# Second attention: the order in which the transfers of the query and key stacks walk their rows

## The chip, the cores and the metric

The kernel runs on one core of a Trainium2 chip. The metric is the time of one execution on the device in microseconds (us), smaller is better. TensorE is called PE below, VectorE DVE, ScalarE ACT, GpSimd POOL and SyncE SP; SP computes nothing and issues transfers (DMAs).

## What is computed

Four layers follow each other, each with a residual and a layer norm: an attention over 16 batches of 512 tokens, a routed feed-forward layer, a second attention, another routed feed-forward layer. The change touches the second attention alone:

```
q = q.reshape(B, S, HEADS, HEAD_DIM)      # 16 heads of 8
k = k.reshape(B, S, HEADS, HEAD_DIM)
logits = jnp.einsum('bihd,bjhd->bhij', q, k) * scale + pos_bias[None]
attn = jax.nn.softmax(logits, axis=-1)
out = jnp.einsum('bhij,bjhd->bihd', attn, v).reshape(B, S, D)
```

## The kernel before

The program has five stages; `attention_two` is the third. It works through 16 batches (`bodies`), each of 4 groups (j = 0 to 3) of 4 heads. A group has 16 tiles (4 heads times 4 blocks of tokens), so a batch has 64.

The query and the key are float32. They are split into three bfloat16 parts each (`split`), whose sum is the value, and the product of query and key is made of the parts that matter: high, middle and low key with the high query, the same with the middle query, high and middle key with the low query. That is 8 pairs of parts, and with a head dimension (`HD`) of 8 it makes 64 rows to contract over. `kst` and `qst` ("stacks") hold these 64 rows of keys and queries, for two heads of a pair on the two halves of the 128 partitions (`HALF`). They are filled through memory: `put_parts` writes the parts to `parts_d`, and `stack(s, j)` reads them back into the rows of group j of batch s. There is one `kst` and one `qst` for all batches.

`stack` issues 12 transfers on SP's queue: for each of two halves three for `kst` and three for `qst`, of 24, 24 and 16 rows (3, 3 and 2 parts times 8 dimensions) of 2 KB each. For `kst` the source walks over the parts; for `qst` it names one part again and again, with a step of 0 (`walks` is False). In the kernel before the rows of a transfer are ordered part first, head dimension second. All twelve signal `stack_in{j}`.

On SP a body runs, in this order: `stack(s, 3)` (from batch 1 on), the load for batch s+2, `tops(s, 1)`, `put_parts(s+1)`, `stack(s+1, 0)`, `tops(s, 2)`, the store of batch s-1, `stack(s+1, 1)`, `tops(s, 3)`, `clear_rows` (2 MB of zeros), `stack(s+1, 2)`, `tops(s+1, 0)`. Ahead of the bodies stand `put_parts` and all four `stack` of batch 0, and behind them `tops(0, 0)`. SP does these strictly one after the other, with their waits.

`tops(s, j)` carries the maxima of the rows of scores: it waits until DVE has made `mT` (`m_ready`, L1786), writes it to `tops_d`, waits for that to land, and reads it with four transfers into `line` (named `spread_line` in the profile).

PE runs over 32 slots of two tiles in each body. In each slot it makes `scores` (L1419, c_s) for tiles 32 ahead, then `below` (L1427) and `biased` (L1437, c_u) for the tiles of the slot, and `values` (L1451, c_o). DVE reads the scores and keeps their maxima (L1781), ACT the exponentials (L1628). Three waits tie PE to SP: `scores` of the first tile of a group waits for `stack_in{j}`, `biased` of the first tile of a group waits for `m_in{j}` of `tops`, and, the other way round, `stack(s, j)` waits for the last `biased` of group j of the batch before, since it overwrites what that reads.

Of the kernel before, what the change touches and what calls it, by code (L numbers as in the profile page):

```python
# [20 lines left out]
NB, N, W = 16, 512, 128  # L21
T = N // P
H, A = 16, 64
# [5 lines left out]
HD = W // H  # L29
# [45 lines left out]
def need(eng, sem, n):  # L75

    if not (isinstance(n, int) and n <= 0):
        eng.wait_ge(sem, n)


def apart(eng, passed):


    eng.sem_inc(passed, 1)
# [1029 lines left out]
def attention_two(nc, g, keep):  # L1114
# [4 lines left out]
    PARTS = 3  # L1119
    HALF = P // 2  # L1120
    PAIRS = H // 2
    GP = G // 2
# [14 lines left out]
    def sem(name):  # L1137
        return g.sem(f"c_{name}")

    with ExitStack() as ctx:  # L1140
        def sb(name, shape, dt=F32):
            return ctx.enter_context(nc.sbuf_tensor(f"c_{name}", shape, dt))
# [15 lines left out]
        rows = sb("rows", [P, T], U32)  # L1158
        st = sb("st", [P, T, 6])
# [86 lines left out]
        with nc.Block() as block:  # L1246

            @block.sync
            def _(sp):
# [15 lines left out]
                def stack(s, j):  # L1265

                    for w in range(2):
                        sp.wait_ge(sem(f"parts_out{w}"), 16 * s.b + 16)
                        apart(sp, sem("sp_passed"))
                    need(sp, sem("u_ps"), ALL * (s.b - 1) + TILES * (j + 1))  # L1270
                    apart(sp, sem("sp_passed"))
                    part = P * N
                    for half in range(2):
                        for st, w, walks in ((kst, 1, True), (qst, 0, False)):
                            for a in range(PARTS):
                                rows = HD * (PARTS if a < PARTS - 1 else PARTS - 1)
                                src = bass.AP(io["parts_d"].tensor,
                                              (2 * s.par + w) * PARTS * part + (0 if walks else a * part) + (half * PAIRS + j * GP) * N,
                                              [[part if walks else 0, rows // HD], [H * N, HD], [1, GP * N]])
                                at_row = HALF * half + a * PARTS * HD  # L1280
                                sp.dma_start(st[at_row:at_row + rows, GP * j:GP * j + GP, :].rearrange("r h n -> r (h n)"), src
                                             ).then_inc(sem(f"stack_in{j}"), 16)

                def tops(s, j):
# [23 lines left out]
                def body(s, on):  # L1308
                    if not isinstance(s.b, int) or s.b > 0:
                        stack(s, 3)  # L1310
                    if on.front:
                        load(s.ahead().ahead())
                    tops(s, 1)
                    if on.nxt:
                        put_parts(s.ahead())
                        stack(s.ahead(), 0)
                    tops(s, 2)
                    if on.tail:
                        store(s.back())
                    if on.nxt:  # L1320
                        stack(s.ahead(), 1)
                    tops(s, 3)
                    clear_rows(sp, "zs_d", s.b, io, sem("rows_clear"))
                    if on.nxt:
                        stack(s.ahead(), 2)
                        tops(s.ahead(), 0)
# [977 lines left out]
```

## Time and profile before

| | us |
|---|---|
| median of 3 runs | 2276.47 |
| the runs | 2275.68, 2276.47, 2283.36 |
| the profiled execution | 2270.51 |
| its span (first to last instruction) | 2268.7 |

The stage of the second attention runs from about 762 to 1990 us of the span. In the profile "c_" stands ahead of its tiles. An SP row of the timeline gives the time at which SP began to issue a transfer, and how long the issuing took; the transfer itself goes on behind it. SP rows of equal names that follow each other are merged into one ("x3"). A wait is shown as idle time in brackets with what ended it. L84 is the line at which SP waits inside a helper.

### The profile page before, as it was taken

To read this page: it belongs to the slowest core of one execution; us is meant where nothing else is said; L and a number is where in the kernel's file an instruction comes from. 1 tells how busy PE (TensorE), PEld (TensorE's weight loads), DVE (VectorE), ACT (ScalarE), POOL (GpSimd) and SP (SyncE) were. 2 spreads that over 40 slices of the span, in tenths; PEclk is the share of its full clock that TensorE was granted. 3 is DMA by queue.
4 is the path that set the end of the run, shared out by engine and by line. 5 is a ranking of instruction groups with operands and counts; after the bars stand their busy time and mean duration, and the time that the engine had idled before them with its cause. 6 is when DMAs were issued, how large, how long until landed. Compare 5 with 4: busy or idle time off the path is not lost. (4 is left out here: it accounts for less than half of the span.)

```text
span 2268.7 us, 46879 instructions
## 1 busy us (share of the span) xinstructions
PE 1857.9 (82%) x15436; PEld 953.6 (42%) x15436; DVE 1481.3 (65%) x4594; ACT 1076.7 (47%) x2723; POOL 800.9 (35%) x811
## 2 busy tenths in 40 slices
PE   8477878777568588898898988988888999679896
PEld 6255556555446323333333333333333333246554
DVE  6268878887521376786778777786677777233277
ACT  3355655556123235555555555555555565323221
POOL 4458888888510212122221222122221220100166
PEclk9689999999789779999999999999999999889999
DMA  3553322332168323332333234332333332144333
GB/s 110 161 186 107 108 87 89 110 107 96 35 190 242 113 78 108 94 114 74 110 98 111 70 110 116 95 114 72 109 95 113 86 97 82 59 134 163 127 98 98
DMA packets 147093, 247.66 MB, mean 109 GB/s; under 512 B 20628, under 2 KB 49316, under 8 KB 146356
## 3 DMA queue, kind: packets, MB, share of 16 engines
q1 hardware_dynamic: 137828, 220.80, 31.7%
q0 software_dynamic: 9072, 24.41, 3.9%
q8 instruction: 105, 1.72, 0.3%
q14 instruction: 88, 0.72, 0.1%
HBM read 198.16 MB, written 121.96 MB: 141 GB/s over the span
## 5 line engine op out<-in xcount | busy, mean ns | idle before, releaser
L1781 DVE CUSTOM_DVE_ANT_0 c_sums<-c_s,bias 128x512 f32<-128x512 f32 x1024 | 663.5, 686 | 249.1 <-PE c_s L1419 176.5
L1628 ACT ACTIVATE c_pT<-c_u 128x512 f32<-128x512 f32 x1024 | 571.7, 596 | 510.7 <-PE c_u L1437 425.6
L1437 PE MATMUL c_u<-spread_line,c_pick 128*32 128x512 bf16 x4096 | 325.1, 395 | 38.5 <-DMA spread_line<-tops_d 38.4
L1451 PE MATMUL c_o<-c_pT,c_vst 128*32 128x256 f32 x4096 | 319.5, 389 | 14.5 <-ACT c_pT L1628 11.3
L1419 PE MATMUL c_s<-c_kst,c_qst 64*128 64x512 bf16 x1024 | 242.5, 402 | 23.5 <-DVE c_tops L1781 18.7
L1427 PE MATMUL c_u<-c_qst,c_kst 64*128 64x512 bf16 x1024 | 227.9, 388 | 25.3 <-issue 12.7
L521 ACT ACTIVATE v<-a_bank,gain 128x64 f32<-128x64 f32 x768 | 165.7, 344 | 54.4 <-DVE vp L735 54.3
L1451 PEld LDWEIGHTS c_o<-c_pT,c_vst 128*32 128x32 f32 x4096 | 122.3, 112 | 139.0 <-issue 30.4
L1375 POOL DMA_INDIRECT zs_d<-c_xs,c_slot x64 | 63.2, 988 | 303.9 <-DMA zs_d<-in_zeros 255.1
L387 PE MATMUL a_bank<-wv,xT 128*128 128x512 f32 x256 | 154.6, 691 | 18.9 <-ACT v L521 14.4
L1437 PEld LDWEIGHTS c_u<-spread_line,c_pick 128*32 128x32 bf16 x4096 | 62.1, 95 | 240.8 <-issue 191.7
L588 POOL TENSOR_TENSOR q<-q,vp 128x1024 f32<-128x1024 f32 x48 | 125.0, 2603 | 104.7 <-DVE vp L735 103.6
L1419 PEld LDWEIGHTS c_s<-c_kst,c_qst 64*128 64x128 bf16 x1024 | 59.1, 93 | 214.8 <-DVE c_tops L1781 104.5
L599 POOL TENSOR_TENSOR s<-q,v 128x1024 f32<-128x1024 f32 x48 | 143.0, 2979 | 0.2
L529 ACT COPY oT<-a_bank 128x512 f32<-128x512 f32 x128 | 69.5, 586 | 148.4 <-PE a_bank L408 148.3
L735 DVE TENSOR_TENSOR vp<-a_bank,ez 128x512 f32<-128x512 f32 x96 | 64.9, 687 | 102.1 <-PE a_bank L387 100.3
L416 PEld LDWEIGHTS a_bank<-wo,oT 128*128 128x128 f32 x1024 | 123.8, 195 | 14.3 <-issue 14.3
L416 PE MATMUL a_bank<-wo,oT 128*128 128x128 f32 x1024 | 126.2, 277 | 0.0
L751 DVE TENSOR_TENSOR o<-o,r 128x1024 f32<-128x1024 f32 x64 | 124.3, 1961 | 0.0
L2075 POOL DMA_INDIRECT e_routed<-us_d,rows x64 | 62.8, 981 | 171.9 <-POOLq L2191 154.3
L408 PE MATMUL a_bank<-ident,o 128*128 128x128 f32 x512 | 79.8, 306 | 52.9 <-DVE o L751 52.2
L1364 POOL TENSOR_TENSOR c_rstd<-c_ve,minus_half 128x4 f32<-128x4 f32 x16 | 16.7, 1045 | 278.6 <-DVE c_ve L1750 278.6
(263 smaller groups left out, 2900.3 us busy)
## 6 DMA issues: line engine op xcount, KB each, us to landing
xs_d<-in_zeros SPq DMA_DIRECT2D x16, 2048.0 KB
zs_d<-in_zeros SPq DMA_DIRECT2D x16, 2048.0 KB
spread_line<-tops_d SPq DMA_DIRECT2D x256, 64.0 KB
parts_d<-c_parts SPq DMA_DIRECT2D x32, 384.0 KB
c_kst<-parts_d SPq DMA_DIRECT2D x256, 48.0 KB
c_qst<-parts_d SPq DMA_DIRECT2D x256, 48.0 KB
d_w<-in_wd SPq DMA_DIRECT2D x24, 384.0 KB
b_w<-in_wb SPq DMA_DIRECT2D x24, 321.0 KB
```

Source lines behind the costliest of these rows:

```text
L387: nc.tensor.matmul(v_ps[h][:], xT[s.par][:, t, :], wv[:, 512 * h:512 * h + 512], start=True, stop=True).then_inc(sem("v_ready"), 1)
L416: mm = nc.tensor.matmul(y_ps[:, t * W:(t + 1) * W], oT[t % 2][:, k, :], wo[:, k, :], start=(k == 0), stop=(k == HA // P - 1))
L521: ins = nc.scalar.activation(dst[:, h * A:(h + 1) * A], v_ps[half][:, k * A:(k + 1) * A], ACT.Copy, scale=gain[s.par][:, t, h:h + 1])
L588: nc.gpsimd.tensor_tensor(q[:, t, :], q[:, t - 1, :], vp[t % 2][:], ALU.add).then_inc(sem("q_ready"), 1)
L599: nc.gpsimd.tensor_tensor(s1[s.par][:, t, :], q[:, t - 1, :], v2[t % 2][:], ALU.add).then_inc(sem("s1_ready"), 1)
L751: v.tensor_tensor(heads(o[t % 2][:]), heads(o[t % 2][:]), r[s.par][:, t, :].unsqueeze(2).to_broadcast([P, H, A]), ALU.mult).then_inc(sem(" ...
L1419: nc.tensor.matmul(s_ps[bank_of(n)][:], qst[rows_of(h), h // 2, t * P:(t + 1) * P], kst[rows_of(h), h // 2, :], start=True, stop=True).the ...
L1427: nc.tensor.matmul(u_ps[bank_of(n)][:], kst[rows_of(h), h // 2, c * P:(c + 1) * P], qst[rows_of(h), h // 2, :], start=True, stop=False, sk ...
L1437: mm = nc.tensor.matmul(u_ps[bank_of(n)][ARRAY * k:ARRAY * (k + 1), :].rearrange("k (t q) -> k t q", t=T), pick[:, c, k, :], line[:, G * j ...
L1451: mm = nc.tensor.matmul(o_ps[ARRAY * i:ARRAY * (i + 1), half * 2 * P:(half + 1) * 2 * P], vst[s.par][:, c, f:f + ARRAY], pT[r % 2][:, i, h ...
L1628: nc.scalar.activation(pT[n // G % 2][:, n % G, :], u_ps[bank_of(n)][:], ACT.Exp).then_inc(sem("exp_done"), 1)
L1781: v.tensor_tensor_reduce(sums[n % 2][:], s_ps[bank_of(n)][:], bias, 1.0, -3.0e38, ALU.add, ALU.max, top_s[j % 2][:, k:k + 1]).then_inc(sem ...
```

## The change

The source of each transfer of `stack` is described with the head dimension outermost and the part second, instead of the part outermost and the head dimension second. `kst` and `qst` are reordered in the same way, so each product sums the same 64 terms in another order. The number of transfers, their sizes and their destinations stay.

```
-                                rows = HD * (PARTS if a < PARTS - 1 else PARTS - 1)
+                                n = PARTS if a < PARTS - 1 else PARTS - 1
                                 src = bass.AP(io["parts_d"].tensor,
...
-                                              [[part if walks else 0, rows // HD], [H * N, HD], [1, GP * N]])
+                                              [[H * N, HD], [part if walks else 0, n], [1, GP * N]])
                                 at_row = HALF * half + a * PARTS * HD
-                                sp.dma_start(st[at_row:at_row + rows, GP * j:GP * j + GP, :].rearrange("r h n -> r (h n)"), src
+                                sp.dma_start(st[at_row:at_row + n * HD, GP * j:GP * j + GP, :].rearrange("r h n -> r (h n)"), src
```

No engine but SP has another order, and on SP no instruction moves: what changes is the form of some. Below, a row is a transfer with its line, what it writes and reads, and the form of its destination (rows x elements of 2 bytes; a 1 between them is a dimension that the destination is given to match a source of three dimensions).

SP ahead of the bodies, the parts of batch 0 (`parts_d`) and the first half of `stack(0, 0)`, before:

```order
L1262 DMA parts_d<-c_parts 128x3x512 x2
L1281 DMA c_kst<-parts_d 24x1024 x2
L1281 DMA c_kst<-parts_d 16x1024
L1281 DMA c_qst<-parts_d 24x1x1024 x2
L1281 DMA c_qst<-parts_d 16x1x1024
```

The same place after:

```order
L1262 DMA parts_d<-c_parts 128x3x512 x2
L1281 DMA c_kst<-parts_d 24x1x1024 x2
L1281 DMA c_kst<-parts_d 16x1x1024
L1281 DMA c_qst<-parts_d 24x1x1024 x2
L1281 DMA c_qst<-parts_d 16x1x1024
```

Before, the source of `kst` is one even walk over 24 (or 16) rows, since a part is exactly 8 rows further on than the part ahead of it: two dimensions fall into one. With the head dimension outermost they don't, and `kst` gets the form that `qst` has had.

SP in a body, the second half of `stack(s+1, 1)`, then `tops(s, 3)` and the zeros, before:

```order
L1281 DMA c_kst<-parts_d 24x1024 x2
L1281 DMA c_kst<-parts_d 16x1024
L1281 DMA c_qst<-parts_d 24x1x1024 x2
L1281 DMA c_qst<-parts_d 16x1x1024
L1290 DMA tops_d<-c_mT 16x256
L1300 DMA spread_line<-tops_d 8x4x1024 x4
L172 DMA zs_d<-in_zeros 128x8x512
```

And after:

```order
L1281 DMA c_kst<-parts_d 24x1x1024 x2
L1281 DMA c_kst<-parts_d 16x1x1024
L1281 DMA c_qst<-parts_d 24x1x1024 x2
L1281 DMA c_qst<-parts_d 16x1x1024
L1290 DMA tops_d<-c_mT 16x256
L1300 DMA spread_line<-tops_d 8x4x1024 x4
L172 DMA zs_d<-in_zeros 128x8x512
```

Nothing moved; `tops` stands behind the same twelve transfers.

## Rows read from the trace of the kernel before

**Rows 1.** The page, part 1: busy time and share by engine.
```profile
PE 1857.9 (82%) x15436; PEld 953.6 (42%) x15436; DVE 1481.3 (65%) x4594; ACT 1076.7 (47%) x2723; POOL 800.9 (35%) x811
```
**Rows 2.** Busy time by stretch (us, then PE, PEld, DVE, ACT, POOL, clock, DMA share, GB/s).
```profile
788.00:860.00 72.00, 56.72 (x411) 15.92 (x411) 48.38 (x163) 23.47 (x49) 12.20 (x15) 0.73 0.29 77
860.00:1900.00 1040.00, 926.92 (x10146) 348.51 (x10146) 775.31 (x2867) 580.13 (x1179) 234.59 (x261) 0.97 0.35 100
```
**Rows 3.** Waits of PE, 860 to 1900 us: us in total, times, longest.
```profile
PE c_u L1437 <- DMA spread_line<-tops_d: 26.3, 16, 3.5
PE c_s L1419 <- DVE c_tops L1781: 17.0, 27, 2.7
```
**Rows 4.** Waits of PE, 788 to 860 us.
```profile
PE c_u L1437 <- DMA spread_line<-tops_d: 7.8, 2, 4.7
...
PE c_s L1419 <- DMA c_qst<-parts_d: 0.8, 1, 0.8
```
**Rows 5.** Line 1281, issues on SP: duration in ns, min/median/max.
```profile
L1281 SPq DMA_DIRECT2D c_kst<-parts_d x384: 4/357/1478, 788.5 to 1902.8; - x192
L1281 SPq DMA_DIRECT2D c_qst<-parts_d x384: 619/689/870, 789.6 to 1904.7; - x192
```
**Rows 6.** Other lines that issue on SP, the same columns.
```profile
L1300 SPq DMA_DIRECT2D spread_line<-tops_d x256: 88/301/545, 818.9 to 1942.9; - x128
...
L172 SPq DMA_DIRECT2D zs_d<-in_zeros x16: 667/677/697, 867.4 to 1943.2; - x16
...
L177 SPq DMA_DIRECT2D zs_d<-in_zeros x1: 648/648/648, 820.2 to 820.2; - x1
...
L320 SPq DMA_DIRECT2D bias_d<-line_d x16: 855/2952/4026, 48.9 to 91.2; - x16
```
**Rows 7.** DMA packets while one stack is filled, 1053.3 to 1062.5 us.
```profile
DMA packets 353, 0.54 MB, mean 59 GB/s; under 512 B 96, under 2 KB 96, under 8 KB 352
...
q1 hardware_dynamic: 352, 0.52, 17.7%
```
**Rows 8.** Timeline of SP at the stage's start: first and last pieces of four stacks.
```profile
788.46 1.13 SPq L1281 DMA_DIRECT2D c_kst<-parts_d  x3
789.63 2.24 SPq L1281 DMA_DIRECT2D c_qst<-parts_d  x3
...
814.16 2.08 SPq L1281 DMA_DIRECT2D c_qst<-parts_d  x3
816.42 0.31 SPq L1290 DMA_DIRECT2D tops_d<-c_mT  x1
```
**Rows 9.** Timeline of DVE, 811 to 817 us: the maxima of group 0, batch 0.
```profile
812.37 0.27 DVE L1786 TENSOR_TENSOR c_mT<-c_misc,c_mT 16x128 bf16<-16x128 f32 x1
```
**Rows 10.** Timeline of PE: the first scores, the first biased, group 2 of batch 0.
```profile
798.72 1.03 PE L1419 MATMUL c_s<-c_kst,c_qst 64*128 64x512 bf16 x3 [0.85 <-DMA c_qst<-parts_d]
...
824.62 1.04 PE L1437 MATMUL c_u<-spread_line,c_pick 128*32 128x512 bf16 x8 [4.67 <-DMA spread_line<-tops_d]
...
856.37 0.62 PE L1437 MATMUL c_u<-spread_line,c_pick 128*32 128x512 bf16 x8 [3.17 <-DMA spread_line<-tops_d]
```
**Rows 11.** Timeline of SP ahead of group 2, batch 0.
```profile
846.22 2.09 SPq L1281 DMA_DIRECT2D c_qst<-parts_d  x3
848.49 0.31 SPq L1290 DMA_DIRECT2D tops_d<-c_mT  x1
```
**Rows 12.** Waits of SP, 860 to 1900 us.
```profile
SPq L84 <- DVE c_mT L1786: 118.7, 46, 5.2
```
**Rows 13.** Timeline of SP, a group 3 and a group 2 late in the stage.
```profile
1731.26 2.09 SPq L1281 DMA_DIRECT2D c_qst<-parts_d  x3
1736.66 0.31 SPq L1290 DMA_DIRECT2D tops_d<-c_mT  x1
...
1786.05 2.09 SPq L1281 DMA_DIRECT2D c_qst<-parts_d  x3
1789.45 0.31 SPq L1290 DMA_DIRECT2D tops_d<-c_mT  x1
```
**Rows 14.** Timeline of PE at the same two groups.
```profile
1743.39 0.61 PE L1437 MATMUL c_u<-spread_line,c_pick 128*32 128x512 bf16 x8 [1.35 <-DMA spread_line<-tops_d]
...
1797.15 0.61 PE L1437 MATMUL c_u<-spread_line,c_pick 128*32 128x512 bf16 x8
```

## The prediction

> **What bounds the kernel now.** I began with the page's busy shares: PE is the busiest engine [rows 1]. Cut by stretch, the steady part of the second attention keeps PE busy for 926.92 of 1040 us, ahead of DVE with 775.31; the first 72 us of the stage are looser, 56.72 us busy [rows 2]. So in this stage a microsecond counts when PE loses it. The second view is therefore PE's waits. Of what this change touches, the steady part shows one wait: `biased` for the transfers of `tops`, 26.3 us in 16 waits, about one in each batch, and none for `kst` or `qst` [rows 3]. At the start of the stage there are two such waits for `tops`, 7.8 us, and one of 0.8 us for a stack [rows 4]. The landing of the stacks is thus hardly waited for. But SP issues a stack's twelve transfers one after the other ahead of nearly every `tops`, so the time that the *issuing* takes can reach PE by way of `tops`. The last view is thus SP's timeline: is SP early or late when DVE has the maxima ready?
>
> **The price of issuing.** A `kst` transfer takes SP 0.357 us, a `qst` transfer 0.689 us (0.619 at the least) [rows 5]. They have the same rows of 2 KB and differ in form: the source of `kst` is one even walk, that of `qst` has two dimensions against a destination that has one. Three `qst` with the gaps between take 2.09 us, three `kst` between 1.1 and 1.2, and a whole stack 6.65 us (four stacks: 788.46 to 814.16 + 2.08 = 816.24, or 27.8 us with the waits between them [rows 8]). After the change all twelve have two dimensions against one. No row shows that form with 8 outermost. The bounds are the nearest rows [rows 6]: `spread_line`, which has 8 outermost on both sides and equal dimensions, 0.301 us; the transfers of zeros, 0.648 and 0.677 us; `bias_d`, with 7 outermost, whose first and cheapest issue took 0.855 us (the others queue up behind its own packets). I take 0.65, between `qst`'s cheapest and its median, as `qst` is the nearest form; its 24 and 16 rows (0.69 and 0.62) have 3 and 2 outermost, and 8 may go like either. With gaps of 0.045 us a stack is then 12 x 0.695 = 8.3 us, +1.65 us. Ends: 12 x 0.345 = 4.1 us (-2.5) and 12 x 0.90 = 10.8 us (+4.2).
>
> **The landings.** The transfers of `qst` spread their rows over more of the 16 DMA engines, those of `kst` over fewer. A stack moves 256 rows with 96 small packets beside them in 9.2 us, 17.7% of the engines' time [rows 7]: 0.177 x 16 x 9.2 / 352 = 0.074 us a packet. Were the last transfer of a stack to put 2 rows on an engine instead of 8, the stack would land 6 x 0.074 = 0.4 us sooner behind its issue. In the steady part nobody waits for that, as no such wait stands in [rows 3]; at the start it can give back 0.4 of the 0.85 us that the first scores wait [rows 10]. I leave it out of the sum, as the issue ahead of it grows by more.
>
> The Trainium skill (DMA: Bandwidth & Descriptors, "Why a DMA increments its semaphore by 16 and not by 1") states that such a transfer runs on as many engines as the largest number up to 16 that divides the outermost dimension of both sides. That makes 12, 12 and 16 for `kst` and 3, 3 and 2 for `qst`, twice 48 small packets, and the trace agrees with its 96 [rows 7]; it makes 8 for every transfer after. By that rule alone one would forecast a gain.
>
> **The sum, place by place.**
> 1. *Start of the stage.* The four stacks of batch 0 stand in a row ahead of `tops(0, 0)`. They end at 816.24; DVE had the maxima at 812.37 + 0.27 = 812.64 [rows 9], 3.6 us earlier, and SP goes on at 816.42 [rows 8]. PE starts `biased` 8.2 us later, at 824.62, after 4.67 us of waiting that this transfer ended [rows 10]. So SP is on the path here, and it grows by 4 x 1.65 = 6.6 us. PE's first scores start some 1 us later too, but DVE then has 3.6 us in hand. Nothing covers the 6.6 us: everything after follows from PE's first `biased`.
> 2. *Group 2 of batch 0.* `stack(1, 0)` ends at 848.31, `tops` follows at 848.49, without a wait in between [rows 11], and PE waits 3.17 us for it [rows 10]. Another 1.65 us.
> 3. *The steady part.* Here SP is early: it waits for DVE's maxima 46 times, 118.7 us in all, 2.6 us on average [rows 12]. A stack that takes 1.65 us longer eats into that. At group 3, where PE waits once in a batch (1.35 us at 1743.39 [rows 14]), SP is done at 1733.35 and begins `tops` at 1736.66: 3.3 us, of which 0.17 is the step itself; no cost [rows 13]. Group 2 is the tightest: at 1788.14 to 1789.45 SP had 1.1 us in hand, and there 0.5 us would come through; PE didn't wait at that group and has some tenths of its own [rows 13, 14]. In that stretch I count five groups with less than 1.65 us in hand (1.1 to 1.6), some 1.5 us of lateness together, of which PE's own room takes a third: +1.0 us. Group 1 has 2.4 us in hand and as much again on PE's side, group 0 more.
>
> Queued behind the longer stacks on SP are also the load for the batch after next, the store and the zeros; PE and POOL show no wait that a delay of 1.65 us there would lengthen on the path to PE.
>
> Sum: 6.6 + 1.65 + 1.0 = +9.25 us. On the profiled execution (2270.51 us, its span 2268.7 and 1.8 around it) that gives 2279.8; the median of the runs stands 6.0 us above the profiled one, and gives 2276.47 + 9.25 = 2285.7 us, +0.4%.
>
> **The rivals.**
> - *The form is dear with more engines.* If issuing pays for each outermost step in this form, as 0.62 for 2, 0.69 for 3 and 0.855 for 7 could be read, a stack is 10.8 us, +4.2. Then the start costs 16.8, group 2 of batch 0 4.2, and in the steady part group 2 comes out late by 4.2 - 2.6 = 1.6, about 1.1 on PE, and group 3 by 4.2 - 3.1 = 1.1, in 14 batches each: 31 us. Total +52, 2328 us. It starts to bite where a stack passes 9.3 us. Against it speak the zeros: 16 and 128 outermost at 0.65 and 0.68 [rows 6].
> - *Faster: 8 outermost is the cheap form.* If what makes `qst` dear is 3 and 2 as outermost dimension, and not the second dimension, all twelve cost what `spread_line` costs, 0.301 us [rows 6], and a stack is 4.1 us. SP then passes the start 10 us sooner, but DVE's maxima hold it at 812.64: 3.6 us gained, 0.8 with earlier first scores, 2.5 at group 2 of batch 0, nothing in the steady part, where DVE sets the time of `tops`. -6.9 us, 2269.6. It decides for faster from a mean issue below 0.51 us. Against it: the zeros have powers of two outermost and are dear.
> - *Nothing to be seen.* `kst` stays at 0.36 us and `qst` gets no dearer, or its gain and `kst`'s loss cancel; the landing gives 0.4 us: 2276. This is also where the skill's rule on engines alone would lead, since no wait of PE but the first hangs on a stack's landing.
>
> **How the numbers follow.** The forecast's price (0.62 to 0.70, +7 to +11.5 us) has 62%, the dear form 14%, the cheap form 6%, nothing to be seen 16%, something else 2%. The range leaves out the dear form's end and little below: 2274 (an execution's scatter under "nothing") to 2298 (a stack of 9.3 us: 4 x 2.65 + 2.65 + 5, and a few us of scatter). A measurement of this kernel can tell about 0.5%, 11.4 us, from no change. Within that lie the cheap form, nothing, and four fifths of the forecast; slower by more are the rest of it and the dear form: slower 0.28, same 0.70, faster 0.02.
>
> **What would show it.** In the profile after: `kst`'s median issue at line 1281 near 0.65 us (0.36: nothing; 0.9: dear; 0.3: cheap), `qst`'s near 0.65 too; SP's last stack of batch 0 ending near 823 instead of 816.24, PE's first `biased` near 831 with some 11 us of waiting; PE's waits for `spread_line` in 860 to 1900 us (shifted) at 27 to 29 us; small packets beside a stack again 96. The prediction falls if the issue price stays outside 0.5 to 0.75, or if PE makes up for a late start later in the batch.

## The result

The changed kernel takes 2298.39 us (median of 4 runs, 2291.08 to 2299.05), the kernel before 2276.07 us (4 runs, 2275.42 to 2283.36). The ratio is 1.0083, 95% interval 1.0054 to 1.0112. It is slower by more than can be confused with no change, and the 22.3 us are 2.4 times the 9.25 that were forecast. On two other chips the same pair gave 1.0122 (1.0089 to 1.0155) and 1.0120 (1.0084 to 1.0156); these intervals overlap with the first.

The profiled execution took 2291.08 us (span 2289.2), 20.6 us more than that of before. Issuing at line 1281, after (duration in ns, min/median/max), beside [rows 5]:

```profile
L1281 SPq DMA_DIRECT2D c_kst<-parts_d x384: 484/650/1617, 794.7 to 1921.9; - x192
L1281 SPq DMA_DIRECT2D c_qst<-parts_d x384: 642/643/1356, 797.0 to 1923.9; - x192
```

`kst` went from 0.357 to 0.650 us, `qst` from 0.689 to 0.643. A stack of twelve takes 8.28 us (median of 64) instead of 6.68. Waits of PE, first from 794 to 872 us, then from 872 to 1912 us, which answer to [rows 4] and [rows 3]:

```profile
PE c_u L1437 <- DMA spread_line<-tops_d: 13.8, 2, 10.9
...
PE c_s L1419 <- DMA c_qst<-parts_d: 0.7, 1, 0.7
```
```profile
PE c_u L1437 <- DMA spread_line<-tops_d: 34.4, 24, 2.9
PE c_s L1419 <- DVE c_tops L1781: 18.6, 30, 1.7
```

The longest of the first group grew from 4.7 to 10.9 us, and in the steady part there are 24 waits with 34.4 us instead of 16 with 26.3. SP's own waits in the steady part (872 to 1912 us) show where its time in hand went: 50.5 us in 32 waits for DVE's maxima, against the 118.7 us in 46 of [rows 12].

```profile
SPq L84 <- PE c_u L1437: 101.0, 28, 9.8
SPq L84 <- DMA parts_d<-c_parts: 65.6, 28, 4.5
SPq L84 <- DMA tops_d<-c_mT: 62.8, 40, 3.3
SPq L84 <- DVE c_mT L1786: 50.5, 32, 5.2
```

The start of the stage in the timelines of SP, DVE and PE, after, beside [rows 8 to 10]:

```profile
794.72 2.25 SPq L1281 DMA_DIRECT2D c_kst<-parts_d  x3
797.01 2.02 SPq L1281 DMA_DIRECT2D c_qst<-parts_d  x3
...
827.54 2.02 SPq L1281 DMA_DIRECT2D c_qst<-parts_d  x3
829.73 0.35 SPq L1290 DMA_DIRECT2D tops_d<-c_mT  x1
```
```profile
818.49 0.27 DVE L1786 TENSOR_TENSOR c_mT<-c_misc,c_mT 16x128 bf16<-16x128 f32 x1
```
```profile
836.98 1.04 PE L1437 MATMUL c_u<-spread_line,c_pick 128*32 128x512 bf16 x8 [10.89 <-DMA spread_line<-tops_d]
```

SP now ends the four stacks at 829.56, 10.8 us behind DVE's maxima (818.76); it was 3.6 us.

**Where the time is.** The stage cut at points of the timelines (us): from the issue of the first load of the stage to the first `kst`, from there to the first `biased`, from that to the one of batch 1, from that to the one of batch 15, and from there to the last store. The chips are numbered in the order of use; "old form" is the row order of before.

| kernel, chip | stage begins | to first kst | to first biased | to batch 1 | batch 1 to 15 | first kst to last store |
|---|---|---|---|---|---|---|
| before, 1 | 762.4 | 26.1 | 36.2 | 65.5 | 1009.7 | 1183.4 |
| after, 1 | 768.6 | 26.1 | 42.3 | 65.8 | 1014.7 | 1197.1 |
| start_only, 2 | 782.0 | 26.1 | 42.6 | 66.2 | 949.2 | 1131.1 |
| after_again, 2 | 771.7 | 26.2 | 42.6 | 66.2 | 967.0 | 1148.7 |
| before_again, 3 | 766.8 | 26.1 | 37.0 | 66.9 | 940.2 | 1116.2 |
| after_third, 4 | 768.0 | 26.2 | 42.0 | 65.8 | 969.9 | 1149.7 |

On chip 1, 13.7 of the 20.6 us lie inside the stage: 6.1 at its start and 5.0 between batches 1 and 15, 2.3 from the first `biased` of batch 15 on. 6.2 us lie ahead of it, in stages that the change doesn't touch.

### The profile page after: what moved, and what is told of

Its sections match the earlier page's. It is cut to its first block and busy times, and to the rows that moved or that the text cites. A ratio compares the mean times of both kernels' runs of the same rounds, so it can differ in the third digit from the quotient of the medians.

```text
span 2289.2 us, 46879 instructions
## 1 busy us (share of the span) xinstructions
PE 1866.4 (82%) x15436; PEld 959.7 (42%) x15436; DVE 1485.3 (65%) x4594; ACT 1079.8 (47%) x2723; POOL 801.2 (35%) x811
## 5 line engine op out<-in xcount | busy, mean ns | idle before, releaser
L1419 PE MATMUL c_s<-c_kst,c_qst 64*128 64x512 bf16 x1024 | 242.9, 404 | 24.8 <-DVE c_tops L1781 20.2
L416 PEld LDWEIGHTS a_bank<-wo,oT 128*128 128x128 f32 x1024 | 128.9, 202 | 14.4 <-issue 14.4
L751 DVE TENSOR_TENSOR o<-o,r 128x1024 f32<-128x1024 f32 x64 | 132.2, 2085 | 0.0
L416 PE MATMUL a_bank<-wo,oT 128*128 128x128 f32 x1024 | 131.0, 284 | 0.0
L1364 POOL TENSOR_TENSOR c_rstd<-c_ve,minus_half 128x4 f32<-128x4 f32 x16 | 16.7, 1045 | 275.2 <-DVE c_ve L1750 275.2
```

The source lines that it names most:

```text
L416: mm = nc.tensor.matmul(y_ps[:, t * W:(t + 1) * W], oT[t % 2][:, k, :], wo[:, k, :], start=(k == 0), stop=(k == HA // P - 1))
L751: v.tensor_tensor(heads(o[t % 2][:]), heads(o[t % 2][:]), r[s.par][:, t, :].unsqueeze(2).to_broadcast([P, H, A]), ALU.mult).then_inc(sem(" ...
L1419: nc.tensor.matmul(s_ps[bank_of(n)][:], qst[rows_of(h), h // 2, t * P:(t + 1) * P], kst[rows_of(h), h // 2, :], start=True, stop=True).the ...
```

## The experiments

Every kernel below was timed beside the kernel before on the same chip (2, 3 or 4, as the tables say), and each ratio is to that. The table is worked out from their timelines in one way: for groups 1 to 3 of batches 1 to 14, **in hand** is the time from the end of SP's last issue ahead of `tops` to the end of DVE's L1786 (negative where SP is late), **write to read** the time from the start of the issue of `tops_d` to that of the first `spread_line`, both means in us, and **PE waits** the sum of PE's idle time just ahead of the group's first `biased`. Where the text gives a mean for group 0, it is over batches 1 to 15.

| kernel, chip | in hand, g1 | g2 | write to read, g1 | g2 | PE waits g1 | g2 | g3 |
|---|---|---|---|---|---|---|---|
| before, 1 | 1.95 | 2.28 | 1.85 | 1.58 | 0.0 | 0.3 | 24.1 |
| after, 1 | 0.25 | -0.36 | 2.63 | 2.01 | 0.3 | 8.1 | 24.4 |
| start_only, 2 | 1.98 | 0.07 | 2.04 | 2.66 | 4.5 | 7.4 | 24.0 |
| after_again, 2 | 0.27 | -1.77 | 2.56 | 2.00 | 8.4 | 20.7 | 25.4 |
| after_load_moved, 2 | 0.70 | -1.28 | 1.82 | 2.09 | 1.9 | 14.0 | 24.8 |
| before_again, 3 | 1.94 | 0.24 | 1.97 | 2.32 | 3.8 | 3.4 | 23.8 |
| before_padded, 3 | 0.75 | -1.74 | 2.93 | 3.04 | 13.1 | 34.8 | 24.8 |
| eight_parts, 3 | 6.12 | 1.20 | 1.91 | 2.11 | 4.6 | 3.1 | 25.0 |
| after_third, 4 | 0.25 | -1.69 | 2.56 | 2.06 | 9.9 | 20.4 | 24.4 |
| issue_only, 4 | 0.21 | -1.79 | 3.01 | 2.59 | 13.0 | 28.8 | 25.5 |

### Twice the same kernels: after_again, after_third, before_again

> The changed kernel once more, with more rounds, since its profiled execution is 20.6 us longer and 6.3 of these lie ahead of the second attention, in stages that the change doesn't touch. Theory (SP's issue time, all inside the second attention: start +6, steady part +8): ratio 1.005 to 1.007, and the stage begins at 762 to 764 us as before. Rival (something of the whole program is slower after the change, such as its placement in memory): the stage begins near 768 us again and the ratio is 1.008 to 1.010.

> The changed kernel once more, so that it shares a chip with the next ones. By the two calls so far (ratios 1.008 and 1.012 on two chips): 1.008 to 1.014, PE's waits for spread_line in the steady part 8 to 26 us above those of the kernel before.

> The kernel before, unchanged, for a trace of it from the same chip as the other kernels of this call. Ratio 1.000 within its interval by every theory. Its use: the second attention from the first biased of batch 1 to that of batch 15 takes as long as with the old form in start_only (949 us on that chip, 1010 us on the first one), if the chip's own pace explains the difference between the two chips.

The changed kernel gave 1.0122 (1.0089 to 1.0155) and 1.0120 (1.0084 to 1.0156), above what the first expectation's theory and its rival allowed; the kernel before against itself 0.9982 (0.9963 to 1.0002). The stage of the changed kernel began at 771.7 us in after_again, where 762 to 764 and 768 were expected, and at 768.0 in after_third; but kernels that are the same up to there began it anywhere from 760.0 to 783.4. So the 6.2 us ahead of the stage on chip 1 are scatter of the stages ahead, and nothing of the change. The loss on chip 2 is inside the stage: between batches 1 and 15 the changed kernel takes 967.0 us where start_only, which has the old form there, takes 949.2.

Those chips run this part quicker (67 to 69 us a batch against 72), before and after. In the kernel before, SP has 0.24 us in hand at group 2 on chip 3 and 2.28 on chip 1, and as much at groups 1 and 3 on both within 0.2 us. PE's waits at group 2 grow by 13.3 us on chip 2 (start_only to after_again) and by 7.8 on chip 1. That fits a smaller room for the longer stacks on the quicker chips, but the ratios of chips 1 and 2 differ by 0.4% with an uncertainty of as much, so that the loss is larger there isn't shown by the runs.

### One part alone: start_only

```
-                                              [[H * N, HD], [part if walks else 0, n], [1, GP * N]])
+                                              [[H * N, HD], [part if walks else 0, n], [1, GP * N]] if s.b == 0 else
+                                              [[part if walks else 0, n], [H * N, HD], [1, GP * N]])
```

> The new row order for the four stacks of batch 0 alone, the old one for all later batches. Theory: four stacks of 8.3 instead of 6.65 us stand on the path once: first biased +6.2 us against the stage's begin, the steady waits of PE for spread_line stay at 26 us, ratio 1.0027 (+6 us). Rival (a slower engine split, 8 engines for all, matters for landings in every batch): most of the loss is in the later batches, and this kernel is at +1 us or less.

Ratio 1.0024 (1.0000 to 1.0047), 5.3 us; from the first `kst` to the first `biased` 42.6 us, as in after_again, against 37.0 in before_again. The start's term holds on its own. PE's steady waits for `spread_line`, 26 us in the expectation, are 35.9 in the table's groups: that number was chip 1's. The rest of the change's 1.2% on that chip comes from later batches.

### SP on the path at the start: after_stack3_moved

```
-                for j in range(GROUPS):
+                for j in range(GROUPS - 1):
                     stack(at(0), j)
                 tops(at(0), 0)
+                stack(at(0), GROUPS - 1)
```

> The changed kernel with the last stack of batch 0 issued behind the first tops instead of ahead of it. Its rows are wanted only some 20 us later. Theory: SP is 10.8 us late at the first tops; one stack less ahead of it takes 8.3 us off, PE's wait at the first biased falls from 10.9 to some 2.7 us and the time by 8 us against the changed kernel: ratio to the kernel before 0.999 to 1.004. Rival (the start's delay is made up for later in the batch): the wait goes, the time stays.

Ratio 1.0087 (1.0060 to 1.0114), above the 0.999 to 1.004 that were expected, since the changed kernel itself stands at 1.0122 on this chip and not at 1.008. It is 0.35% or 7.8 us below after_again on the same chip, with an uncertainty of 0.4%, so the runs alone don't show the gain; the traces do. The first `biased` comes 33.0 us after the first `kst` instead of 42.6; 1.6 us of that are given back in batch 0 (67.8 instead of 66.2 us to batch 1). Waits of PE up to 870 us in after_again, then in this kernel:

```profile
PE c_u L1437 <- DMA spread_line<-tops_d: 11.3, 1, 11.3
```
```profile
PE c_u L1438 <- DMA spread_line<-tops_d: 4.6, 2, 3.2
```

Of the 4.6 us 1.4 are at the first `biased`. So in these traces only those 1.6 us of the start are made up for later, and the change's delay there goes by a move of twelve transfers that nobody wanted yet.

### The load ahead of the small write: after_load_moved

```
-                    if not isinstance(s.b, int) or s.b > 0:
-                        stack(s, 3)
                     if on.front:
                         load(s.ahead().ahead())
+                    if not isinstance(s.b, int) or s.b > 0:
+                        stack(s, 3)
```

> The changed kernel with the load of 256 KB for the batch after next issued ahead of the stack of group 3, instead of right ahead of the tops of group 1. Theory: with longer stacks SP comes to that tops without slack, so its small write is issued 0.9 us behind the load instead of 2.5 and lands 1.8 to 3.6 us later; this and two longer stacks in a row make SP late at group 2. With the load out of the way the write takes 1.3 us again, PE's waits for spread_line in the steady part fall from 34.4 us in 24 waits to 26 to 29 in 16 to 18, and the time by 5 to 8 us against the changed kernel. Rival (it is the longer stacks alone): the waits fall by 2 us or less.

This came out of a comparison of SP's timeline at group 1. The kernel before, and after, in the same batch:

```profile
1332.43 0.41 SPq L1252 DMA_DIRECT2D c_x<-x_d  x1
1334.75 0.31 SPq L1290 DMA_DIRECT2D tops_d<-c_mT  x1
1336.35 1.30 SPq L1300 DMA_DIRECT2D spread_line<-tops_d  x4
...
1344.08 1.12 SPq L1281 DMA_DIRECT2D c_kst<-parts_d  x3
```
```profile
1345.88 0.44 SPq L1252 DMA_DIRECT2D c_x<-x_d  x1
1346.51 0.32 SPq L1290 DMA_DIRECT2D tops_d<-c_mT  x1
1348.90 1.30 SPq L1300 DMA_DIRECT2D spread_line<-tops_d  x4
...
1356.19 2.07 SPq L1281 DMA_DIRECT2D c_kst<-parts_d  x3
...
1362.43 2.02 SPq L1281 DMA_DIRECT2D c_qst<-parts_d  x3
1364.64 0.34 SPq L1290 DMA_DIRECT2D tops_d<-c_mT  x1
```

Before, the small write of `tops` stands 2.3 us behind the load of 256 KB and its read can start 1.6 us later. After, it stands 0.6 us behind, and that takes 2.4 us. Everything up to the next stack shifts by that, the stack is 1.6 us longer itself, and SP reaches the `tops` of group 2 late, without a wait. PE then waits where it did not (timeline of PE, after):

```profile
1373.14 0.61 PE L1437 MATMUL c_u<-spread_line,c_pick 128*32 128x512 bf16 x8 [0.89 <-DMA spread_line<-tops_d]
```

With the load moved the ratio is 1.0041 (1.0018 to 1.0064), 0.8% or 18 us below after_again, and batches 1 to 15 take 949.2 us, as in start_only. The write to read of group 1 falls from 2.56 to 1.82 us, PE's waits at groups 1 and 2 from 29.1 to 15.9 us. These numbers are above what was expected in us, and the count of waits (35, with 46.9 us) is not down to the expected 18; that had been reckoned from chip 1. The move also takes 0.5 us of issuing out of the chain, and how the 18 us divide between that and the quicker write isn't shown. The rival, that it is the longer stacks alone, is out: their length is the same in both (8.27 us), and PE's waits at groups 1 and 2 fell by 13 us where it allowed 2. The DMA packets show the write held up: at group 1 of batches 1 to 13 the last packets ahead of it end 1.6 us after its issue in after_again (0.4 in after_load_moved), and its own last packet at 1.9 us (1.2).

### The form without the 8 engines: before_padded

```
-                        sp.dma_start(io["parts_d"][s.par, w].rearrange("a p n -> p a n"), parts[w][:]
+                        sp.dma_start(io["parts_d"][s.par, w, :, 0:P].rearrange("a p n -> p a n"), parts[w][:]
...
-                    part = P * N
+                    part = (P + 1) * N
...
-"parts_d": ([2, 2, 3, P, N], BF16)
+"parts_d": ([2, 2, 3, P + 1, N], BF16)
```

> The kernel before with one unused row block between the parts in memory. The row order stays part first, but the key's source is no longer one even walk, so its transfers get the form of the query's, on 3 and 2 engines instead of 12 and 16; the 8 engines of the change are not in it. Theory (the issue time alone counts): kst issues at 0.69 and 0.62 us, a stack takes 8.5 us, the first biased comes 7 us later after the stage's begin, batches 1 to 15 take as much longer as in the changed kernel, ratio 1.009 to 1.014 on the chip of the last call. Rival (the number of engines or the later landing matters): the ratio differs from the changed kernel's by 0.4% or more, either way.

Issuing at line 1281:

```profile
L1281 SPq DMA_DIRECT2D c_kst<-parts_d x384: 619/672/881, 786.1 to 1906.8; - x192
L1281 SPq DMA_DIRECT2D c_qst<-parts_d x384: 619/675/1004, 788.5 to 1908.9; - x192
```

The stack is 8.44 us, as long as the changed kernel's 8.28 within 0.2, and the ratio is 1.0386 (1.0357 to 1.0415): three times the change's loss. My theory at that point, that the issue time alone counts, fell. Waits of SP in the steady part, in before_again and then here:

```profile
SPq L84 <- DMA tops_d<-c_mT: 110.3, 61, 3.5
```
```profile
SPq L84 <- DMA tops_d<-c_mT: 151.6, 55, 5.7
```

SP waits longer for its own small write to land, 2.8 instead of 1.8 us on average, up to 5.7. With 3, 3 and 2 engines for each transfer of `kst` and `qst`, those few still work through the stack when the write arrives: at group 2 the stack's last packet ends 2.4 us after the write's issue (1.3 in before_again, 1.0 in after_third), and the write's own last packet at 2.4 (1.6 and 1.3). At group 0, behind the zeros, the write to read takes 5.3 us on average here and 3.1 in before_again. Not all of the 66 us between batches 1 and 15 are waits for `spread_line`, which grow by 49 us. PE's busy time grows by 15, at a granted clock of 0.978 instead of 0.993; whether the waits brought the clock down isn't shown.

### SP's time alone: issue_only

```
                                sp.dma_start(st[at_row:at_row + rows, GP * j:GP * j + GP, :].rearrange("r h n -> r (h n)"), src
                                             ).then_inc(sem(f"stack_in{j}"), 16)
+                                if walks:
+                                    for _ in range(5):
+                                        apart(sp, sem("sp_passed"))
```

> The kernel before (old form, 12, 16, 3 and 2 engines) with five instructions that only count a semaphore up behind each kst transfer on SP, some 1.4 to 2.0 us a stack: SP's time as in the changed kernel, the transfers as before. before_padded had the changed kernel's issue time and lost 3.9% instead of 1.2%, with PE waiting 80 us for spread_line and the small write of tops landing later behind the packets of 3 engines. Theory A (issue time alone is the change's loss, the 8 engines give nothing): the same ratio as after_third within 0.3%. Theory B (the spread over 8 engines gives back a part, since the write of tops no longer queues behind the stack on the first three engines): 0.4% or more above after_third, with a mean time from the write of tops to the read of it for group 2 of 2.5 us or more instead of 2.0. Theory C (fewer engines for kst cost something): below after_third by 0.3% or more.

The ratio is 1.0250 (1.0221 to 1.0279), beside 1.0120 (1.0084 to 1.0156) of after_third on the same chip. The stack takes 8.38 us (median), the changed kernel's 8.27; in hand at groups 1 and 2 they are alike (means 0.21 and -1.79 here, 0.25 and -1.69 there). Write to read at group 2 is 2.59 us against 2.06, at group 1 3.01 against 2.56, at group 0 2.63 against 2.18, and PE's waits for `spread_line` in the steady part are, here and then in after_third:

```profile
PE c_u L1440 <- DMA spread_line<-tops_d: 73.1, 41, 4.2
```
```profile
PE c_u L1437 <- DMA spread_line<-tops_d: 57.7, 43, 3.2
```

That is theory B. At group 2 the last packet of the stack ends 1.9 us after the issue of the write here and 1.0 in after_third, and the write's last packet at 2.0 and 1.3. The change is two things of opposite sign: the time that SP issues, about +2.5%, and the spread of the stacks over 8 engines, about -1.3% (29 us, give or take 10), which the write of `tops` feels. In the traces the stage is 25 us longer here; between batches 1 and 15 it is 16.7, of which 5.4 are PE's busy time at a clock of 0.979 instead of 0.984. The pauses stand behind `kst` alone and not evenly, and the +2.5% hold for the old spread, so the split is good to some tenths of a per cent, not better.

### Both moves: before_both_moved, after_both_moved

> The kernel before (old, cheap form) with both moves tried on the changed one: the last stack of batch 0 behind the first tops, and the load for the batch after next ahead of the stack of group 3. Theory: at the start SP was 3.6 us late and is so no more, -3.6 us or a bit more; in the steady part SP has 2.4 us in hand at group 1 already, so the write behind the load is mostly undisturbed and the move gives 0 to 3 us. Ratio 0.996 to 0.999. Rival (the write is hindered before the change as well, on this faster chip): 5 us or more of the steady part go too, ratio below 0.996.

> The changed kernel with both moves, the last stack of batch 0 behind the first tops and the load ahead of the stack of group 3. The moves took 0.35% and 0.8% off it one by one. Theory (two separate places of the sum): together -1.1 to -1.2%, a ratio to the kernel before of 0.999 to 1.003. Rival (they overlap): 1.003 or above.

On the kernel before the two moves give 0.9958 (0.9937 to 0.9979). What the trace shows of it is all at the start: 30.5 us from the first `kst` to the first `biased` instead of 37.0, and nothing between batches 1 and 15 (945.1 against 940.2 us). So the rival's part of the steady stretch isn't there, though the ratio is just at its bound. SP there waits for DVE, and the small write is alone (timelines of SP and DVE):

```profile
814.82 2.09 SPq L1281 DMA_DIRECT2D c_qst<-parts_d  x3
819.73 0.31 SPq L1290 DMA_DIRECT2D tops_d<-c_mT  x1
821.19 1.31 SPq L1300 DMA_DIRECT2D spread_line<-tops_d  x4
```
```profile
819.30 0.27 DVE L1787 TENSOR_TENSOR c_mT<-c_misc,c_mT 16x128 bf16<-16x128 f32 x1
```

The gain is larger than the 3.6 us of the expectation, which was chip 1's. On this chip SP was 5.2 us late in before_again, and its write to read took 2.82 us; here it takes 1.46, as the write no longer follows a stack directly. Together that is the 6.5 us. On the changed kernel they give 1.0030 (1.0005 to 1.0054), 0.9% below after_third; one by one they had given 0.35% and 0.8%. Theory and rival meet at that value, and it doesn't tell them apart; batches 1 to 15 take 948.7 us instead of 969.9.

### Fewer transfers: eight_parts, eight_load_moved

The parts stand in memory as eight blocks instead of three, in the order of the 64 rows, and a stack is 4 transfers of one even walk (the six writes of the parts aren't shown):

```
+                            src = bass.AP(io["parts_d"].tensor, (2 * s.par + w) * 8 * part + (half * PAIRS + j * GP) * N,
+                                          [[H * N, HALF], [1, GP * N]])
```

> The kernel before with the parts written to memory eight times over, in the order in which the stacks take them, so that each stack is 4 transfers of 64 rows in one even walk instead of 12. Theory: a stack takes SP 1.5 us instead of 6.65; the writes of the parts are six transfers instead of two, three of them with a repeated source at 0.67 us (+2.4 us), and land later (2 MB instead of 0.8 MB). SP is early at every tops: start -3.6 us and -2.5 at group 2, PE's waits for spread_line that remain are those in which DVE sets the time; ratio 0.994 to 0.998. Rival (the larger writes hold up the first stack of a batch by more than the shorter issue gives): 1.000 or above, with waits for kst or qst.

> The parts written eight times and stacks of 4 transfers (eight_parts, 0.996), and the load ahead of the stack of group 3. With SP 6 us early at group 1 the load is long done when the small write starts, so the move should give little: 0.994 to 0.997. Rival (the five waits of PE at group 1 that eight_parts still has come from the load): those waits go, another 3 to 5 us, 0.993 or below.

0.9959 (0.9943 to 0.9975), and with the load moved 0.9966 (0.9946 to 0.9985), no different; PE still waits 3.0 us at group 1, against 4.6, so these waits didn't come from the load alone. The issues are dearer than I reckoned, and a stack takes 2.4 us and not 1.5:

```profile
L1283 SPq DMA_DIRECT2D c_kst<-parts_d x128: 444/588/1533, 788.8 to 1822.0; - x128
L1283 SPq DMA_DIRECT2D c_qst<-parts_d x128: 581/596/1649, 789.4 to 1822.7; - x128
```

SP has 6 us in hand at group 1, and still batches 1 to 15 take 941.2 us where before_again takes 940.2: more time in hand than before bought nothing there. What is left are PE's 25 us at group 3, which no kernel here changed and where DVE's maxima set the time. The gain is the start's: 28.6 us from the first `kst` to the first `biased`, though the larger writes of the parts put that `kst` 2 us later. Of all kernels tried this and before_both_moved are the fastest, by 0.4%, and not to be told apart.

## Why the prediction was right in its mechanism and short in its size

**The price: right.** `kst` 0.65 us was forecast, the median is 0.650; the stack 8.3 us, it is 8.28. The number of outermost steps hardly mattered in this form: with 3 and 2 outermost in before_padded and with 8 after, it is 0.62 to 0.69. The dear and the cheap rival are out. Form isn't all, though: an even walk takes 0.36 us with 16 or 24 rows and 0.59 with the 64 rows of eight_parts. Of the other signs that were named, the end of the last stack (829.56, or 823.3 when shifted by the 6.26 us that the stage's first `kst` came later), the first `biased` (830.7 so), its wait of 10.9 us and the 96 small packets came; PE's steady waits, 27 to 29 us, did not: they were 34.4.

**The start: right in size, with two errors that partly cancel.** 6.6 us were forecast, 6.1 measured between the first `kst` and the first `biased` on chip 1, 5.3 us by start_only's ratio. The four stacks alone grew by 7.05 us, from 27.78 to 34.84; the write to read behind them fell from 2.47 to 1.81 us, and the rest up to PE's `biased` by 0.3. The shorter write to read stood in no term of the sum.

**Group 2 of batch 0: wrong, +1.65 forecast, 0.** PE waits there 2.95 us and not 3.17 + 1.65. SP begins that `tops` 1.4 us later against PE's first `biased`, but its write to read takes 1.71 us (862.21 to 863.92) instead of 2.58 (848.49 to 851.07): the write behind the evenly spread stack lands sooner. In the packets, the last one of the stack ends 1.96 us after the write's issue before and 1.01 after, and the last one of the write 0.03 us behind it both times. The step that failed is the one that put the spread at nothing because nobody waits for a stack's landing: it had the stack 0.4 us sooner behind its issue and left that out. Measured here it is 0.95 us, and somebody waits for what comes behind the stack on the same engines.

**The steady part: wrong, +1.0 forecast.** On chip 1 PE's waits grew by 8.1 us and the stretch by 5.0; on chip 2 the stretch grew by 17.8 (after_again against start_only). Two steps failed. I measured what SP has in hand at group 1 to the end of the stack and got 2.4 us; behind the stack stands the load, and past it there were 1.95. And I took "SP isn't late" for "no cost": of those 1.95 us 0.25 were left, so SP was late at only three of 14 groups 1, but the write came within a microsecond of the load and took 0.8 us longer to be read back, which with the next stack's 1.6 us made SP late at 9 of 14 groups 2. after_load_moved shows this part by taking it away. The five tight groups were counted rightly, though one of them is a group 1; with 1.65 us a stack their lateness adds up to 1.0 us and not to 1.5.

**The sum.** +9.25 us was forecast, the stage shows 13.7 and the runs 22.3, which puts the median of 2298.39 us at the very end of the range, 2298. The price had been given 62%, and +7 to +11.5 us with it: the price came and that stretch did not. A loss beyond 11.4 us had been given 0.28, half of it to the dear form, and it came by a way that no rival named. The range allowed 21.5 us; the 27 us of chips 2 and 4 lie beyond it, so that it comes this near on chip 1 is in part luck. Of the profiled execution's 20.6 us, 6.2 are scatter of the stages ahead. What of the runs' 22 us on chip 1 is such scatter and what is not can't be told from one trace; on chip 2 the stage accounts for some 23 of the loss of 27 us (17.6 from start_only to after_again, and 5.6 at the start from before_again, which is chip 3's); of chip 4 there is no trace of the kernel before. That SP's room can differ from chip to chip was in no step of the sum. Why chips 2 to 4 run a batch in 67 to 69 us where chip 1 takes 72 wasn't settled. Between batches 1 and 15 the kernel before takes 69.5 us more on chip 1 than on chip 3: 34 are PE's busy time, at a granted clock of 0.970 against 0.993, and 38 are idle time of PE, of which waits for ACT's `c_pT`, 23 us, don't stand among chip 3's.

The Trainium skill's rule (DMA: Bandwidth & Descriptors, "Why a DMA increments its semaphore by 16 and not by 1") holds where the runs can show it. While one stack is filled after, from 1300.5 to 1310.4 us, 496 packets of SP's queue stand in the trace, 112 of them small. The store issued just ahead has 128 rows and 16 small ones; without them it is the 352 with 96 small ones of [rows 7], as 12 transfers on 8 engines each make it.

```profile
DMA packets 497, 0.80 MB, mean 80 GB/s; under 512 B 112, under 2 KB 112, under 8 KB 496
...
q1 hardware_dynamic: 496, 0.79, 24.3%
```

By the rule that is the same 96 as before the change, so this count alone doesn't test it. before_padded does: 3, 3 and 2 engines for all transfers make 32 small packets a stack, 64 fewer, in 64 stacks 4096 fewer. The packets of SP's queue in the whole execution, in before_again and in before_padded, differ by just that:

```profile
q1 hardware_dynamic: 137828, 220.80, 32.8%
```
```profile
q1 hardware_dynamic: 133732, 220.79, 31.0%
```

The gain that I said one would forecast by it alone exists, 1.3% on chip 4. It is covered by twice as much loss in issuing.

## What to carry to other kernels

Issuing a transfer costs its queue's engine time, and the form alone can change that: here 0.36 us for one even walk of 16 or 24 rows and 0.65 us where source and destination have different dimensions. Count it for everything that the queue does next. Then ask two things of a queue that gets slower or faster: what small, waited-for transfer stands behind a large one on the same DMA engines, and whether a wait that still ends in time has moved closer to that large one. Slack is worth reading on more than one chip: group 2 had 2.28 us of it on one and 0.24 on another, in the same kernel.

## What the hardware showed that I had not expected

- A transfer of 64 rows of 2 KB in one even walk took SP 0.588 to 0.596 us to issue, those of 16 and 24 rows 0.36 us.
- What a write of 8 KB (`tops_d`) takes depends on what stands ahead of it. From its issue to that of the read it was 1.8 us on average at group 3, where the stack's last packet ended 1.0 to 2.3 us ahead of it on average; at group 0, behind 2 MB of zeros and a stack, it was 3.15 us in the kernel before, 1.84 in the changed one with its 8 engines, and 5.3 us in before_padded. The change made this step shorter by 1.3 us on average on chip 1, at a group where PE didn't wait before or after.
- The first stages of one and the same code ended anywhere from 760 to 783 us in fourteen traces.
